# Moving the output projection of windowed attention from the end of an odd unit into the next even unit

## The reference, cut to what matters

```
xn  = layernorm(x)                                  # x: 8 batches of 512 rows, 256 columns
qkv = xn @ w_qkv + b_qkv                            # 16 heads of 16
for each window of 128 rows, at a stride of 64:
    probs = softmax(q k^T / sqrt(16));  ow = probs @ v
o   = concat(ow) @ w_out + b_out, its first 512 rows
out = x + o + moe(xn)                               # 8 experts, the best 2 of each token
```

## Time and profile before

| | us |
|---|---|
| median of 3 runs (704.3 to 704.83) | 704.5 |
| the profiled execution | 704.97 |
| its span, first to last instruction | 703.2 |
| busy in the span: TensorE matmuls | 630.0 |
| VectorE | 567.5 |
| ScalarE | 513.2 |
| GpSimd | 281.5 |
| mean granted TensorE clock | 0.981 |

### The profile page before, as it was taken

The page is one execution under the profiler, slowest core; times in us unless marked ns, Lnnn a source line. Parts: engine busy times, 40 slices in busy tenths (PEclk is TensorE's granted clock), DMA queues, the critical chain, the costliest instruction groups (busy, mean ns, idle before and its releaser), DMA issues.

```text
span 703.2 us, 17940 instructions
## 1 busy us (share of the span) xinstructions
PE 630.0 (90%) x5914; PEld 509.7 (72%) x5915; DVE 567.5 (81%) x902; ACT 513.2 (73%) x882; POOL 281.5 (40%) x330
## 2 busy tenths in 40 slices
PE   0786785989999999999999999999999999999985
PEld 0554564765888888888888888888767676666663
DVE  4968899986888888888888888888587979788884
ACT  4554578396787787777877877777577788888885
POOL 3000274033344444444544544444201336666654
PEclk9998789899999999999999999999999999999999
DMA  9795478491111111111111111111178778885740
GB/s 299 263 257 193 110 251 305 121 314 48 53 52 52 60 52 52 59 48 57 53 52 60 52 53 60 52 52 54 38 192 242 180 246 209 262 228 159 207 141 31
DMA packets 66337, 92.62 MB, mean 132 GB/s; under 512 B 6432, under 2 KB 53408, under 8 KB 66272
## 3 DMA queue, kind: packets, MB, share of 16 engines
q1 hardware_dynamic: 57904, 70.56, 33.8%
q0 software_dynamic: 6816, 18.62, 7.9%
q10 hardware_dynamic: 1568, 2.76, 1.2%
HBM read 58.93 MB, written 32.83 MB: 130 GB/s over the span
## 4 chain that ended last, share of the span: by engine, by line
PE 65%; DVE 14%; ACT 10%; issue 7%; POOL 2%; DMA 1%; ACTq 0%; DVEq 0%; POOLq 0%
PE PS L1319 57%; PE PS L1570 4%; DVE SMALL L980 4%; ACT WORK L785 3%; PE PS L1548 2%; DVE XN L1138 2%; DVE WALL L974 2%; ACT QS L780 1%; DMA XN<-in_x 1%; DVE WORK L1049 1%; DVE WORK L1042 1%; ACT WORK L723 1%; DVE WALL L998 1%; ACT SIDE L792 1%; POOL OTS L595 1%
## 5 line engine op out<-in xcount | busy, mean ns | idle before, releaser
L367 DVE TENSOR_TENSOR WS<-WALL,WS 128x1024 fp32r<-128x1024 f32 x134 | 164.4, 1227 | 55.2 <-ACT WS L877 40.8
L1319 PE MATMUL PS<-WS,XTS 128*128 128x512 f32 x804 | 203.9, 402 | 0.0
L1319 PEld LDWEIGHTS PS<-WS,XTS 128*128 128x128 f32 x804 | 146.2, 189 | 30.5
L877 ACT ACTIVATE WS<-WALL 128x1024 fp32r x134 | 141.6, 1056 | 8.8 <-issue 0.3
L1319 PE MATMUL PS<-DOWN_HIGH,HTS 128*128 x568 | 115.9, 289 | 0.8 <-ACT HTS L892 0.8
L595 POOL TENSOR_TENSOR OTS<-SIDE,XN 128x256 f32<-128x256 f32 x30 | 22.8, 761 | 205.2 <-DVE XN L1138 138.5
L1319 PEld LDWEIGHTS PS<-DOWN_HIGH,HTS 128*128 128x128 f32 x568 | 90.9, 188 | 1.6 <-issue 1.5
L980 DVE TENSOR_REDUCE SMALL<-PS 128x8 f32<-128x1024 f32 x64 | 77.5, 1211 | 12.2 <-PE PS L1319 11.9
L785 ACT ACTIVATE WORK<-PS 128x512 f32<-128x512 f32 x128 | 69.4, 595 | 23.6 <-PE PS L1319 20.3
L667 POOL DMA_INDIRECT ys_scratch<-SIDE,SIDX x36 | 43.8, 1218 | 93.2 <-ACT SIDE L908 93.2
L663 POOL DMA_INDIRECT XS<-xn_scratch,GIDX x71 | 71.8, 1011 | 23.0 <-issue 21.3
(11 more groups left out here) (147 smaller groups left out, 1090.9 us busy)
## 6 DMA issues: line engine op xcount, KB each, us to landing
WALL<-in_wexp SPq DMA_DIRECT2D x28, 384.0 KB, 7.1
WALL<-ys_scratch SPq DMA_DIRECT2D x16, 512.0 KB, 7.2
parts_scratch<-WORK SPq DMA_DIRECT2D x32, 240.0 KB, 2.4
QS<-parts_scratch SPq DMA_DIRECT2D x16, 480.0 KB, 4.6
XN<-in_x SPq DMA_DIRECT2D x4, 1024.0 KB, 12.1
xn_scratch<-XN SPq DMA_DIRECT2D x4, 1024.0 KB, 7.3
WALL<-in_x SPq DMA_DIRECT2D x8, 512.0 KB, 5.9
KS<-parts_scratch SPq DMA_DIRECT2D x16, 240.0 KB, 4.1
```

The source lines that it names most:

```text
L367: eng.tensor_tensor(out=WS[:, 1 - k, half, 1], in0=weights, in1=WS[:, 1 - k, half, 0].bitcast(F32), op=ALU.subtract).then_inc(low_ready[ha ...
L877: act.activation(WS[:, 1 - k, half, 0], weights, ACT.Copy).then_inc(high_ready[half], 1)
L1319: return pe.matmul(o, a, b, start=start, stop=stop)
```

## The change

TensorE's `project()` no longer stands at the end of an odd unit. It stands in the next even unit, behind that unit's projection of queries, keys or values and ahead of `scores`. VectorE's `project` moves alike: into the next even unit, behind `take_max()` and ahead of `invert()`. Windows 2 and 3 of a batch are so finished in units 0 and 2 of the next one; in batches 1 and 7, where the batch ends a stage, window 2 is finished behind the last unit. No instruction is added, removed or changed in size.

```diff
--- before.py
+++ after.py
@@ -1203,6 +1203,10 @@
                         split(u)
                     if not (last and u >= UNITS - 3):
                         take_max()
+                    if u in (0, 2) and pending:
+                        project(b - 1, NWIN - 2 + u // 2)
+                    if u in (4, 6):
+                        project(b, u // 2 - 2)
                     if u in (2, 4, 6) or (u == 0 and pending):
                         invert()
                     if first == 0:
@@ -1232,15 +1236,12 @@
                             finish_map()
                     if b == 0 and u == 3:
                         dve.wait_ge(xn_out, 64)
-                    if u == 1 and pending:
-                        project(b - 1, NWIN - 1)
                     if ends(b) and u == UNITS - 1:
                         invert_halves()
-                    if u % 2 == 1 and u > 1:
-                        project(b, u // 2 - 1)
                 if not last:
                     c["W"].add(NWIN)
                 if ends(b):
+                    project(b, NWIN - 2)
                     if not last:
                         for n in range(*DOWN_AT[0:2]):
                             low_down(n)
@@ -1494,6 +1495,8 @@
                             queries_keys(BLOCKS[u])
                         else:
                             values(u - 4)
+                    if u % 2 == 0 and (u > 2 or (b and b != EXTRA)):
+                        project()
                     if u < UNITS - 3:
                         scores(par, u + 3)
                     elif not last:
@@ -1518,9 +1521,8 @@
                         slot_map()
                     if first == 1 and u == MAP_UNIT + 1:
                         pe.wait_ge(map_taken, 1)
-                    if u % 2 == 1 and (u > 1 or (b and b != EXTRA)):
-                        project()
                 if ends:
+                    project()
                     project()
 
             for stage in range(2):
```

## The result

The kernel after takes 712.12 us (median of 4 runs, 712.0 to 713.06) against 704.4 us (4 runs, 703.89 to 704.83): a ratio of 1.0113 with a 95% interval of 1.0095 to 1.013, so it is slower by some 1.1%. The forecast was 713.8. A second measurement, beside other experiments, gave 712.93 against 705.15, 1.0122 (1.0093 to 1.0152). The profiled execution has a span of 710.4 us against 703.2.

A forecast was written before the change was run, and what follows sets the result against it. Bound: a loop from VectorE's reciprocal through GpSimd and ScalarE to `split(2)`. 704.97 + 4.4 (batches 2 to 7) + 4.9 (batch 1) = 714.3 profiled, which stands 0.47 above the median: forecast 713.8 us, range 708.5 to 717.0.

The forecast's parts named there:

- What bounds the kernel: No engine fills a batch, so the order inside it decides; in units 0 to 4 a three-engine loop sets the pace.
- The loop from reciprocal to `split(2)`: VectorE's reciprocal of unit 0, GpSimd's division, ScalarE's chain to `take_part`, then VectorE's split: 6.24 us.
- TensorE's move at 0: Projections moved behind the next unit's projection gain 0; in unit 0 they delay scores, taken as 0, upper end 2.7 us.
- The nine waits: TensorE's waits of 0.59 us for the division in batches 2 to 6: taken as worth 0, at most 5.3 us.
- 0.35 an addition; 1.05 a batch: VectorE's addition ahead of the reciprocal costs 0.35 us in units 0, 2 and 6, 1.05 in each of batches 4 to 6.
- unit 4 free: The addition in unit 4 takes the 0.35 us that unit 3 gave up, so it costs 0.
- The list 2.87 later, its copy 2.7 later: Batch 1, unit 2: `slot_map`'s matmuls wait for a moved addition, starting 2.87 us later; VectorE's `take_map` comes 2.7 later.
- The clock, 2.0: Batch 1: TensorE's clock may fall in the longer pause ahead of `slot_map`, costing 2.0 us, bounds 0 and 4.0.
- matmuls longer than 4.0 us: Sign expected in the profile after: `slot_map`'s 64 matmuls take over 4.0 us, with a granted clock below 1 beside them.
- Batch 0 at 0: VectorE is never idle from batch 0's unit 2 on, so an addition moved there costs and gains nothing.

The follow-up runs named there:

- `add_twice`: Kernel after, with each moved VectorE addition done a second time into a spare buffer, ahead of the real one: 717.87 us, ratio 1.0193.
- `add_behind_inverse`: Kernel after, with VectorE's additions of batches 2 to 7 behind the reciprocal instead of ahead of it: 708.96 us, ratio 1.0066.
- `early_inverse`: Kernel before, with the reciprocals of units 0 and 6 ahead of `split` and `take_max` from batch 2 on: 700.91 us, ratio 0.9939.
- `tensor_only`: Kernel before, with only TensorE's projections moved and VectorE's additions left at the end of odd units: 705.76 us, ratio 1.0024.
- `map_window_back`: Kernel after, with window 3 of batch 0 projected and added at the end of unit 1 of batch 1 again: 710.71 us, ratio 1.0095.
- `map_later`: Kernel after, with the addition that the list of slots waits for moved behind the reciprocal of unit 2 in batch 1: 715.06 us, ratio 1.0164.
- `vector_only`: Kernel before, with only VectorE's additions moved and TensorE's projections left at the end of odd units: 714.86 us, ratio 1.0147.
- `early_stage_only`: Kernel before, with the whole change in batches 0 and 1 alone: 708.27 us, ratio 1.0055.
- `late_stage_only`: Kernel before, with the whole change in batches 2 to 7 alone: 710.89 us, ratio 1.0081.

## Why the prediction was right, and where it wasn't

- **What bounds the kernel.** Right. The loop from reciprocal to `split(2)` takes a delay in full (after, `add_twice`) and gives back what is taken out of it (`add_behind_inverse`, `early_inverse`).
- **TensorE's move at 0.** Right within the whole change, not for the move alone. The nine waits were worth nothing; waits for the maxima and for `W_BANK` took their place. Alone the move costs 1.6 us (0.8 to 2.5, the interval of `tensor_only`); the prediction had up to 2.7 for it as an upper end. The Trainium skill's page "Perfetto Trace Analysis", section "Optimization Strategies", wants the matmul engine kept busy and the engines that block the critical path made faster; here this idling of TensorE wasn't on that path.
- **0.35 an addition; 1.05 a batch.** Right: 1.07 in batches 4 and 5, 1.14 in batches 6 and 7 together, 0.90 in batch 3, 0.3 in batch 2, with unit 4 free. The part in unit 2 hangs on when the split meets GpSimd's division, which the prediction didn't see.
- **The list 2.87 later, its copy 2.7 later.** Right: 2.88 and 2.68, both counted from batch 0's reciprocal of unit 6, and released by VectorE's addition as named. `map_window_back` takes it out, `map_later` lengthens it one for one.
- **The clock, 2.0.** Right in kind, mis-sized. With the list late the granted clock fell to 0.50 in five of seven profiles (`vector_only`, `add_behind_inverse`, `early_stage_only`, `map_later`, `add_twice`), and cost 1.45 to 1.65 us each time; in the two profiles of the kernel after it stayed at 1.00. Two of the five have the instruction order of the kernel after up to the list, so it is a chance of some 1.5 us, not a cost of 2.0, and the promised sign "matmuls longer than 4.0 us" did not show in the profile after.
- **Batch 0 at 0.** Wrong. The prediction's VectorE "that is never idle" does idle at the maxima of unit 6: it waits there for TensorE's scores, 0.17 to 0.34 us in four of the five profiles with the old order there. So the addition of unit 5, ahead of these maxima, filled idle time, and behind them it costs its length. From the reciprocal of unit 4 to that of unit 6 it takes 9.30 us in the kernel before and 9.56 to 9.73 in the other four with the old order, 9.79 and 9.85 with one of the two moves, and 9.97 to 10.26 in the seven with both, so the change costs some 0.5. First `late_stage_only` (old order), then `early_stage_only` (new order), TensorE's scores and then VectorE:

```profile
100.07 1.06 PE L1325 MATMUL PS<-KS,QS 96*128 96x128 bf16 x8
```

```profile
100.65 0.41 DVE L974 TENSOR_TENSOR XN<-PS,BOUT 128x256 f32<-128x256 f32 x1
101.24 1.23 DVE L980 TENSOR_REDUCE SMALL<-PS 128x8 f32<-128x1024 f32 x1 [0.18 <-PE PS L1325]
```

```profile
98.71 1.06 PE L1325 MATMUL PS<-KS,QS 96*128 96x128 bf16 x8
```

```profile
99.90 1.22 DVE L980 TENSOR_REDUCE SMALL<-PS 128x8 f32<-128x1024 f32 x1 [0.63 <-PE PS L1325]
...
101.45 0.42 DVE L974 TENSOR_TENSOR XN<-PS,BOUT 128x256 f32<-128x256 f32 x1
101.78 1.74 DVE L1138 RECIPROCAL XN<-XN 128x256 f32<-128x256 f32 x1
```

The reciprocals of unit 4 start at 93.22 and 91.77 us, so the scores come 6.85 and 6.94 us behind them, and the two reciprocals of unit 6 9.57 and 10.01. Of these 0.44 us 0.33 is the addition. The clock isn't what makes the difference: it is at 0.50 on both sides (eight matmuls take 1.06 us instead of 0.61). Only the kernel before had full clock there. Its 9.30 us are some 0.3 shorter for that, and the 0.86 in the table of stretches are 0.3 more than the change costs.

The terms of the forecast sum to 9.3 us. Without the 2.0 for the clock and with 0.5 for batch 0 they would be 7.8; the medians are 7.7 apart. The forecast is thus 1.7 us too high, and not more because two errors of opposite sign partly cancel. That is luck, and so is some of the closeness of the 7.8: single executions of one kernel lie up to 3.4 us apart (702.66 to 706.07 for the kernel before on one chip).

## What to carry to other kernels

Take an instruction that moves on an in-order engine past the one that starts a loop through other engines, and charge its start-to-start time, 0.34 us here, once for each pass in which nothing idles between them; where another engine runs through without a wait, as over unit 4, charge nothing. A wait on the busiest engine is worth something only if the next wait behind it is not for someone else. Look for one-time steps that wait for everything of a kind, like the list's wait for all of `r_free`: such a step took 2.7 us, more than two whole batches lost. And the idle time in front of a wait is the place for work that another engine is waiting for: the same reading gave a kernel 0.6% faster.

## What the runs showed of the hardware

- The length of the pause ahead of the list did not decide whether TensorE's clock fell there, nor did the order of the instructions: a pause of 2.20 us in `early_stage_only` and of 2.19 in `add_behind_inverse` had it at 0.50, and one of 2.87 in the kernel after, with the same order up to the list, kept it at 1.00. The Trainium skill's page "TensorE: Matmul & The Clock Gate", section "Part 1: The HAM clock gate (the "warmup" mystery)", says that the number of slow matmuls varies from run to run; the profiles agree. In a kernel of 700 us a fall took 1.45 to 1.65 us at the list, and falls at other times shift instructions that the edit doesn't touch (VectorE's split at 74 us came 0.91 us earlier, relative to the first split of batch 0, where the clock was at 0.50 for some 3 us and not for 10).
- A cast of 128x320 took 0.33, 0.64 or 0.76 us, and a 128x8 operation on `MH` 0.17 or 0.65, by what GpSimd did beside it (0.76: the cast at 621.04 in the kernel after, 0.15 us behind the start of a GpSimd addition). An addition put ahead of such an instruction can so cost less than its length, or nothing.
